# Gated cross-attention with a mixture of experts: VectorE's, GpSimd's and SyncE's steps of a loop turn in another order

## The chip, the cores and the metric

The kernel runs on one core of a Trainium2 chip. The metric is the device time of one launch in microseconds. The engines are named PE (TensorE), DVE (VectorE), ACT (ScalarE), POOL (GpSimd) and SP (SyncE, which here only issues DMAs). Each engine works through its own list of instructions in order, and engines are tied to each other by semaphores.

## The reference

32 sequences of 128 tokens, 256 features, 16 heads of 16, 8 experts with 1024 hidden features, all in 32 bits:

```python
x = x + tanh(g_xattn) * attention(layernorm(x), ctx, ctx, w_q, b_q, w_k, b_k, w_v, b_v, w_o, b_o)
# attention: causal softmax(q k^T / 4) v per head, over the 128 tokens of a row, then @ w_o.T + b_o
# ffn(x): logits = x @ Wr + br; top 2 of 8 experts; weights = softmax of the two logits
#         sum over them of weight * (gelu(x @ W1[e] + b1[e]) @ W2[e] + b2[e])
x = x + tanh(g_ffn) * ffn(layernorm(x), W1, b1, W2, b2, Wr, br)
```

## The kernel before

The launch has two parts. `attention_and_routing` does the attention, the second layer norm and the choice of experts for all 4096 tokens, and writes each normalised token into rows of a table in HBM (`xs_dram`) sorted by expert; on the side it turns the experts' weights into scaled pairs of 16 bit numbers. `experts` then runs over 39 tiles of 256 rows. All edits are in the first part.

The first part works in 16 groups g of two sequences (256 tokens). Each engine has a function `it(g, par, half, stays, stayed)` that writes out one turn of the loop, and `loop_over_groups` runs it for g = -2 to 17; `there(g)` says whether a group exists, so that the turns at both ends have only some of the steps. `par` is g mod 2 and chooses the buffer of a pair, `p1` = 1 - par, `g1` = g + 1. A turn has eight slots n = 0 to 7, one for each block of four heads of one sequence. Several groups are in work at once. In turn g:

- group g has its scores in slot n (PE, L906), their maxima for each row (DVE, L753), a cover, that is the mask with the maxima in it (POOL, `affine_select`, L502), the transposed scores with the cover taken off (PE, L964 and L966, two slots later), the exponentials (ACT, L591), and the product with the values (PE, L999, three slots later);
- group g + 1 is prepared. Keys: projection (PE, slot 1), the first of three 16 bit parts (ACT, `first_part`, L570), what is left of it (DVE, `rest`, L682, reads the PSUM bank PJB), the second part (ACT, L609), the third part (DVE, `third`, L694). Queries: the same from slot 3 on. The values' projection (PE, slot 2) overwrites PJB, so it waits for `rest` of the keys (`k_left`). SP copies each part as soon as it is made into the stacked layout that the scores read, six DMAs for the keys and six for the queries (L413);
- group g - 1 is finished: normalisation of the output (`normalise`, L702 and L703), output projection (PE, slots 0 and 4), the second residual (`residual`, L713, which reads `xb` = x + gated bias, made by POOL at L511), its variance, 1/std (POOL, L494), the norm (`norm2`, L722), transposes, and the router's product in slot 7, then logits, mask (L854) and shifted logits (L856);
- group g - 2 gets its places: exponentials, weights, counts (L789 to L806, slot 1), positions (L745, L747) and slots (L811 to L820, slot 2), and POOL scatters its rows by four indirect DMAs (L519);
- one layer of one expert's weights is loaded (SP, L399, into `stage`), squared and summed (ACT, L639, slots 3 to 6), and in the next turn scaled and split into a high half (ACT, L646, slots 1 to 4) and a low half (DVE, L763, four pieces of 512);
- slot 7 also takes the first layer norm's statistics of group g + 2 (DVE, L863 to L870), with 1/std on POOL (L528), and slot 0 of the next turn applies them (L770).

SP's order in a turn is: loads of x and context for group g + 2 (L359, L360; they wait until the buffers are free, that is for `xn_ready`, `xb_ready` and `cT_psum` of group g), the load of weights (it waits for the low halves of the turn before, `w_low`), the copies of keys and of queries, the store of the residual, and from group 8 on a store of the split weights. The order on each engine is written by hand.

## Time and profile before

| | us |
|---|---|
| median of 3 runs | 928.24 (926.72 to 928.42) |
| the profiled execution | 926.99 |
| its span, from the first to the last instruction | 925.2 |
| busy in it: PE, weight loads, DVE, ACT, POOL | 825.1, 743.3, 611.5, 441.2, 354.1 |

The attention part ends at about 454 us, the experts take the rest. In the first part the weights' sum of each turn (L842, end of slot 7) stands at 51.8, 79.2, 103.75 and so on to 430.9, once in each turn. A row of the timeline gives the start, the duration, the engine, line and operation, what it writes and reads, and in brackets how long the engine was idle just before and what ended that. Neighbouring instructions of DVE overlap a little, so one starts before the end of the last. An instruction that stands in its engine waiting for a port counts as busy.

### The profile page before, as it was taken

The numbers are of one execution on the slowest core, as the hardware profiler recorded it, in microseconds if no ns is written. First come the engines' busy times: TensorE is split into PE (matmuls) and PEld (weight loads), VectorE is DVE, ScalarE is ACT, GpSimd is POOL, SyncE is SP. The second block draws the span as 40 slices with busy tenths as digits, with TensorE's granted clock in tenths as the row PEclk, the third lists the DMA queues.
The fourth block names the chain that finished last, engine by engine and source line by source line (L and its number), as shares of the span: only waits on it lengthen the run. The fifth ranks groups of instructions, "written<-read, shape, count | busy, mean of one in ns | idle before, by whom it ended". The sixth has DMA issues, their size and how long they took to land. (4 is left out here: it accounts for less than half of the span.)

```text
span 925.2 us, 24761 instructions
## 1 busy us (share of the span) xinstructions
PE 825.1 (89%) x7472; PEld 743.3 (80%) x7473; DVE 611.5 (66%) x1492; ACT 441.2 (48%) x962; POOL 354.1 (38%) x365
## 2 busy tenths in 40 slices
PE   4599999999999999997259999999999999999990
PEld 3488888888888888887148999999998999999980
DVE  2368988899889989996635556555555555555550
ACT  2146555656555555554034444444455444444440
POOL 2233565554555555654301322332223223322232
PEclk9799999999999999999569999999999999999996
DMA  8876657667667887672577332233233332223222
GB/s 186 151 138 141 165 154 154 139 150 165 160 155 200 207 217 200 189 191 82 183 267 270 61 55 49 49 50 53 48 55 56 50 53 49 49 48 43 24 25 26
DMA packets 87947, 108.80 MB, mean 118 GB/s; under 512 B 12832, under 2 KB 81568, under 8 KB 85664
## 3 DMA queue, kind: packets, MB, share of 16 engines
q1 hardware_dynamic: 72448, 87.17, 37.3%
q0 software_dynamic: 14304, 19.15, 13.3%
q8 instruction: 60, 0.98, 0.4%
q10 hardware_dynamic: 1088, 1.11, 0.4%
q14 instruction: 47, 0.39, 0.2%
HBM read 46.82 MB, written 34.36 MB: 88 GB/s over the span
## 5 line engine op out<-in xcount | busy, mean ns | idle before, releaser
L1228 POOL DMA_INDIRECT out_rows<-yg,xs x78 | 128.0, 1641 | 330.4 <-ACT yg L1270 193.4
L1360 PE MATMUL bank<-xh,wts 128*128 128x256 f16 x1872 | 213.6, 275 | 0.0
L1376 PE MATMUL bank<-wts,hh 128*128 x1872 | 210.6, 273 | 0.0
L1360 PEld LDWEIGHTS bank<-xh,wts 128*128 x1872 | 184.6, 99 | 22.3
L1376 PEld LDWEIGHTS bank<-wts,hh 128*128 128x128 f16 x1872 | 183.2, 98 | 21.2
L1260 ACT ACTIVATE hf<-bank,b1t,gscale 128x256 f32<-128x256 f32 x312 | 154.3, 560 | 24.3 <-PE bank L1360 24.3
L502 POOL TENSOR_SCALAR_AFFINE_SELECT xs<-rowmax 128x512 bf16<-128x512 bf16 x128 | 96.0, 750 | 161.5 <-DVE rowmax L753 147.1
L999 PE MATMUL bank<-va,probs 128*128 128x102 f32 x1024 | 140.6, 279 | 3.8 <-DVE ao L703 3.5
L1270 ACT ACTIVATE yg<-yb,xs 128x256 f32<-128x256 f32 x78 | 35.4, 500 | 199.5 <-DVE yb L1309 184.1
L999 PEld LDWEIGHTS bank<-va,probs 128*128 128x128 f32 x1024 | 125.1, 193 | 5.5 <-issue 3.4
L1299 DVE SCALAR_TENSOR_TENSOR hh<-hf,hscale,hh 128x512 f16<-128x512 f32 x156 | 117.2, 752 | 5.6
L591 ACT ACTIVATE probs<-bank 128x512 f32<-128x512 f32 x128 | 76.4, 597 | 73.3 <-PE bank L966 53.9
L1309 DVE SCALAR_TENSOR_TENSOR yb<-bank,yscale,b_all 128x512 f32<-128x512 f32 x39 | 29.3, 750 | 109.0 <-PE bank L1376 109.0
L753 DVE TENSOR_REDUCE rowmax<-bank 128x4 bf16<-128x512 f32 x128 | 87.6, 685 | 16.3 <-PE bank L906 13.5
L1298 DVE TENSOR_SCALAR hh<-hf,hscale 128x512 f16<-128x512 f32 x156 | 75.5, 484 | 22.1 <-ACT hf L1260 15.6
L519 POOL DMA_INDIRECT token_rows<-pay,slots x64 | 71.7, 1121 | 22.2 <-DVE slots L816 10.8
L964 PE MATMUL bank<-negident,xs 128*128 128x128 bf16 x512 | 73.3, 220 | 6.7 <-POOL xs L502 6.7
L966 PE MATMUL bank<-wts 96*128 96x128 bf16 x512 | 73.5, 220 | 0.0
L1283 DVE SCALAR_TENSOR_TENSOR xh<-bank,xh 128x512 f16<-128x512 f32 x39 | 27.0, 692 | 67.3 <-ACT xh L1251 65.7
L906 PE MATMUL bank<-wts 128*128 128x128 bf16 x512 | 50.3, 221 | 16.7 <-DMA wts<-queries 14.6
L964 PEld LDWEIGHTS bank<-negident,xs 128*128 128x128 bf16 x512 | 49.9, 99 | 10.0 <-POOL xs L502 9.1
L906 PEld LDWEIGHTS bank<-wts 128*128 128x128 bf16 x512 | 40.4, 101 | 20.4 <-issue 17.3
(165 smaller groups left out, 1072.3 us busy)
## 6 DMA issues: line engine op xcount, KB each, us to landing
wts<-in_W SPq DMA_DIRECT2D x16, 1024.0 KB, 8.7
wts<-keys SPq DMA_DIRECT2D x96, 128.0 KB
wts<-queries SPq DMA_DIRECT2D x96, 128.0 KB
xs<-token_rows SPq DMA_DIRECT2D x39, 272.0 KB
split_weights<-wts SPq DMA_DIRECT2D x8, 1024.0 KB
wts<-split_weights SPq DMA_DIRECT2D x8, 1024.0 KB, 7.4
xin<-in_x SPq DMA_DIRECT2D x16, 256.0 KB, 2.8
cin<-in_ctx_in SPq DMA_DIRECT2D x16, 256.0 KB, 3.1
```

What stands on the lines that cost most here:

```text
L502: pool.affine_select(out=cover[n % 4][:, :, :], in_=rowmax[n % 2][:, :].unsqueeze(2).to_broadcast([P, 4, P]), compare_op=ALU.is_ge, fill=M ...
L591: act.activation(probs[q % 4][:, :, :].rearrange("p a q -> p (a q)"), TB[q % 2][:, :], ACT.Exp, scale=float(DK) ** -0.5).then_inc(exp_read ...
L753: dve.tensor_reduce(rowmax[n % 2][:, :], SB[n % 2][:, :].rearrange("p (a k) -> p a k", a=4), AX, ALU.max).then_inc(max_ready, 1)
L906: last = pe.matmul(ps[:, a * P:(a + 1) * P], qfull[par][:, h, tok], kfull[par][:, h, tok], start=True, stop=True)
L964: pe.matmul(ps[:, a * P:(a + 1) * P], cover[m % 4][:, a, :], negident[:, :], start=True, stop=False)
L999: last = pe.matmul(OB[:, h * VA:(h + WIDE) * VA], probs[m % 4][:, a, :], va[i][:, b, h, :].unsqueeze(1).to_broadcast([P, WIDE, VA]), start ...
L1228: pool.indirect_dma_start(out=out[:, :], out_offset=bass.IndirectOffsetOnAxis(ap=numbers, axis=0), in_=yg[m % 2][:, half, :], in_offset=No ...
L1260: last = act.activation(hf[:, c, :], HB[quarter][:, c % 2 * TILE:(c % 2 + 1) * TILE], ACT.Gelu, bias=b1t[:, bass.ds(e, 1), c], scale=gscal ...
L1298: step(dve.tensor_scalar(high, full, hscale[:, bass.ds(e, 1)], None, ALU.mult))
L1299: dve.scalar_tensor_tensor(out=hh[b][:, 1, c, :].rearrange("p c t -> p (c t)"), in0=full, scalar=hscale[:, bass.ds(e, 1)], in1=high, op0=A ...
L1360: last = pe.matmul(HB[c // 2][:, c % 2 * TILE:(c % 2 + 1) * TILE], wts[:, bass.ds(expert[1], 1), at:at + P], xh[b][:, xp, k, :], start=q = ...
L1376: last = pe.matmul(YB[b][:, half * D:(half + 1) * D], hh[b][:, hp, c, half * P:(half + 1) * P], wts[:, bass.ds(expert[0], 1), at:at + D], ...
```

## The change

- DVE: `rest` of the keys stands in slot 1 amid the routing steps of group g - 2, behind `esum`, instead of behind all of them (in turns without such a group it stays at its place).
- DVE: the four pieces of the low half lie in slots 3, 4, 5, 6 instead of 2, 3, 5, 6.
- DVE: `third` of the queries stands in slot 5 behind the maxima instead of at the end of slot 4.
- DVE: in turns 15 and later the second `normalise` stands in slot 2, ahead of the slots' steps, instead of slot 3.
- POOL: the sum x + bias is made in the group's own turn, ahead of slot 2's cover, instead of in slot 6 of the turn before.
- POOL: the third of the four indirect DMAs lies in slot 6 instead of slot 5.
- SP: the load of weights comes first in a turn, ahead of the loads of x and context.

```diff
--- before.py
+++ after.py
@@ -348,6 +348,18 @@
                     return a[bass.ds(g * (GT * P), GT * P), :].rearrange("(b p) d -> p b d", p=P)
 
                 def it(g, par, half, stays, stayed):
+                    if there(g):
+
+                        when(sp, there(g - 2), w_low, (g - 1) * 4)
+                        settled(sp)
+                        e = half
+                        if par == 0:
+                            src = W1[bass.ds(e, 1), :, :].rearrange("a (k p) n -> p (a k) n", p=P)
+                            dst = stage[0].rearrange("p (k n) -> p k n", k=KC)
+                        else:
+                            src = W2[bass.ds(e, 1), :, :].rearrange("a (k p) n -> p (a k) n", p=P)
+                            dst = stage[1].rearrange("p (k n) -> p k n", k=HC)
+                        sp.dma_start(dst, src).then_inc(w_staged[par], 16)
                     if there(g + 2):
 
                         when(sp, there(g), xn_ready, g + 1)
@@ -385,18 +397,6 @@
                         for half in range(2):
                             at = E * REG + half * P
                             load(xs_dram[at:at + P, :], padrow[:, :])
-                    if there(g):
-
-                        when(sp, there(g - 2), w_low, (g - 1) * 4)
-                        settled(sp)
-                        e = half
-                        if par == 0:
-                            src = W1[bass.ds(e, 1), :, :].rearrange("a (k p) n -> p (a k) n", p=P)
-                            dst = stage[0].rearrange("p (k n) -> p k n", k=KC)
-                        else:
-                            src = W2[bass.ds(e, 1), :, :].rearrange("a (k p) n -> p (a k) n", p=P)
-                            dst = stage[1].rearrange("p (k n) -> p k n", k=HC)
-                        sp.dma_start(dst, src).then_inc(w_staged[par], 16)
                     if there(g + 1):
                         for w, src, st, made, dst_ready in (
                                 (1, keys, kst, (k_first, k_second, keys_ready), kst_ready),
@@ -493,6 +493,14 @@
                             pool.wait_ge(var2_ready, (g - 1) * GT + b + 1)
                             pool.tensor_tensor(rs2[:, b:b + 1], mv2[:, b, 1:2], power[:, 0:1],
                                                ALU.pow).then_inc(rstd2_ready, 1)
+                        if n == 2 and there(g):
+
+                            arrived(pool, x_loaded, g, par)
+                            when(pool, there(g - 2), x2_ready, (g - 1) * GT)
+                            pool.wait_ge(bias_ready, 1)
+                            pool.tensor_tensor(xb[par][:, :, :], xin[par][:, :, :],
+                                               bo_all[:, :].unsqueeze(1).to_broadcast([P, GT, D]),
+                                               ALU.add).then_inc(xb_ready, 1)
                         if there(g):
 
                             pool.wait_ge(max_ready, g * QUADS + n + 1)
@@ -503,16 +511,8 @@
                                                in_=rowmax[n % 2][:, :].unsqueeze(2).to_broadcast([P, 4, P]),
                                                compare_op=ALU.is_ge, fill=MASKED, base=0, pattern=[[0, 4], [-1, P]],
                                                channel_multiplier=1).then_inc(cover_ready, 1)
-                        if n == 6 and there(g + 1):
-
-                            arrived(pool, x_loaded, g + 1, 1 - par)
-                            when(pool, there(g - 1), x2_ready, g * GT)
-                            pool.wait_ge(bias_ready, 1)
-                            pool.tensor_tensor(xb[1 - par][:, :, :], xin[1 - par][:, :, :],
-                                               bo_all[:, :].unsqueeze(1).to_broadcast([P, GT, D]),
-                                               ALU.add).then_inc(xb_ready, 1)
-                        if n in (3, 4, 5, 7) and there(g - 2):
-                            b, r = divmod((3, 4, 5, 7).index(n), 2)
+                        if n in (3, 4, 6, 7) and there(g - 2):
+                            b, r = divmod((3, 4, 6, 7).index(n), 2)
                             if n == 3:
                                 pool.wait_ge(slots_ready, g - 1)
                                 settled(pool)
@@ -735,7 +735,8 @@
                             dve.wait_ge(tanh_ready, 2)
                             dve.tensor_scalar(bo_all[:, :], bo_all[:, :], tgx[:, 0:1], None,
                                               ALU.mult).then_inc(bias_ready, 1)
-                        if n == 3 and there(g - 1):
+                        ending = isinstance(g, int) and g >= NG - 1
+                        if n == 3 and there(g - 1) and not ending:
                             normalise(g - 1, 1)
                         if n == 7 and there(g):
                             normalise(g, 0)
@@ -752,11 +753,13 @@
                             when(dve, n >= 2 or there(g - 1), cover_ready, g * QUADS + n - 1)
                             dve.tensor_reduce(rowmax[n % 2][:, :], SB[n % 2][:, :].rearrange("p (a k) -> p a k", a=4),
                                               AX, ALU.max).then_inc(max_ready, 1)
+                        if n == 5 and there(g1):
+                            third(g1, p1, n)
                         if n == 5 and there(g - 1):
                             norm2(g - 1, 1, p1)
-                        if n in (2, 3, 5, 6) and there(g - 1):
-
-                            k = (2, 3, 5, 6).index(n)
+                        if 3 <= n <= 6 and there(g - 1):
+
+                            k = n - 3
                             c = slice(512 * k, 512 * k + 512)
                             dve.wait_ge(w_high, g * 4 - 3 + k)
                             e = half - (1 - par)
@@ -790,7 +793,10 @@
                             for b in range(GT):
                                 step.later(dve.tensor_tensor_scan(cnt[:, b, :], ones8[:, :], msk16[:, b, :], 0.0,
                                                                   ALU.mult, ALU.add))
-                            step(dve.tensor_reduce(esum[:, :], em[:, :, :], AX, ALU.add))
+                            step.later(dve.tensor_reduce(esum[:, :], em[:, :, :], AX, ALU.add))
+                            if there(g1):
+                                rest(g1, n)
+                            step.wait()
                             step.later(dve.reciprocal(erec[:, :], esum[:, :]))
 
                             step.later(dve.tensor_tensor(cm[:, :, :], cnt[:, :, :], msk16[:, :, :], ALU.mult))
@@ -806,6 +812,8 @@
                             step(dve.tensor_tensor(sel[:, :, :, :], over_ranks(cm[:, :, :]),
                                                    rank1[:, :].unsqueeze(1).unsqueeze(3).to_broadcast([P, GT, 8, E]),
                                                    ALU.is_equal))
+                        if n == 2 and there(g - 1) and ending:
+                            normalise(g - 1, 1)
                         if n == 2 and there(g - 2):
 
                             step(dve.tensor_tensor(sel[:, :, :, :], sel[:, :, :, :], over_ranks(pos[:, :, :]), ALU.mult))
@@ -818,7 +826,7 @@
                                                      op1=ALU.add).then_inc(slots_ready, 1)
                             dve.wait_ge(slots_ready, g - 1)
                             step.later(dve.tensor_copy(all_slots[:, bass.ds((g - 2) * GT, GT), :], slots[par][:, :, :]))
-                        if n == 1 and there(g1):
+                        if n == 1 and not there(g - 2) and there(g1):
                             rest(g1, n)
                         if n == 2 and there(g1):
                             third(g1, p1, n)
@@ -834,8 +842,6 @@
                             rest(g1, n)
                         if n == 4 and there(g - 1):
                             residual(g - 1, 1, PJB, p1)
-                        if n == 4 and there(g1):
-                            third(g1, p1, n)
                         if n == 7 and there(g):
 
                             dve.wait_ge(w_total, g + 1)
```

## Rows read from the trace of the kernel before

**Rows 1.** Windows: length, busy PE, PEld, DVE, ACT, POOL; clock, DMA share, GB/s.
```profile
103.75:408.34 304.59, 287.34 (x2679) 262.67 (x2677) 275.17 (x793) 174.65 (x396) 166.46 (x193) 1.00 0.70 173
...
419.80:423.20 3.40, 3.40 (x24) 3.34 (x23) 1.52 (x3) 1.46 (x4) 1.88 (x3) 0.50 0.10 36
```

**Rows 2.** Groups by line, DVE, 20 to 425: busy us, mean ns, idle before.
```profile
L854 DVE TENSOR_TENSOR msk<-lg,mx 128x16 bf16<-128x16 f32 x14 | 14.3, 1022 | 0.5
...
L713 DVE SCALAR_TENSOR_TENSOR x<-bank,tgx,xb 128x256 f32<-128x256 f32 x29 | 13.9, 478 | 11.5 <-PE bank L887 11.5
...
L811 DVE TENSOR_TENSOR sel<-sel,pos 128x128 f32<-128x128 f32 x14 | 10.1, 720 | 0.0
...
L870 DVE TENSOR_SCALAR mv<-mv 128x2 f32<-128x2 f32 x15 | 5.0, 334 | 0.5
...
L672 DVE TENSOR_SCALAR mv<-mv 128x1 f32<-128x1 f32 x29 | 4.5, 154 | 1.0
...
L806 DVE TENSOR_TENSOR sel<-cm,rank 128x128 f32<-128x128 f32 x14 | 4.0, 284 | 0.0
```

**Rows 3.** Timeline, slots 6 and 7: start, duration, instruction, [idle before, releaser].
```profile
203.67 1.50 POOL L519 DMA_INDIRECT token_rows<-pay,slots  x1 [0.17 <-DVE rowmax L753]
...
205.80 1.27 POOL L511 TENSOR_TENSOR xb<-xin,bo_all 128x512 f32<-128x512 f32 x1
...
206.05 1.07 DVE L854 TENSOR_TENSOR msk<-lg,mx 128x16 bf16<-128x16 f32 x1
...
207.02 0.64 POOL L502 TENSOR_SCALAR_AFFINE_SELECT xs<-rowmax 128x512 bf16<-128x512 bf16 x1
```

**Rows 4.** Timeline, slots 1 and 2, of POOL, DVE and PE.
```profile
214.00 0.64 POOL L502 TENSOR_SCALAR_AFFINE_SELECT xs<-rowmax 128x512 bf16<-128x512 bf16 x1 [0.86 <-DVE rowmax L753]
...
214.93 0.15 DVE L796 TENSOR_TENSOR cm<-cnt,msk 128x16 f32<-128x16 f32 x1
...
215.81 0.88 DVE L682 SCALAR_TENSOR_TENSOR k_rest<-bank,bqk,keys 128x256 f32<-128x256 f32 x2
...
216.75 0.48 PE L887 MATMUL bank<-wv_sb,cT 128*128 128x256 f32 x1 [1.04 <-DVE k_rest L682]
```

**Rows 5.** Timeline, slots 4 to 7, of POOL, DVE and PE.
```profile
225.02 0.63 POOL L502 TENSOR_SCALAR_AFFINE_SELECT xs<-rowmax 128x512 bf16<-128x512 bf16 x1 [0.61 <-DVE rowmax L753]
...
225.39 0.48 DVE L713 SCALAR_TENSOR_TENSOR x<-bank,tgx,xb 128x256 f32<-128x256 f32 x1 [0.71 <-PE bank L887]
...
227.28 0.68 DVE L753 TENSOR_REDUCE rowmax<-bank 128x4 bf16<-128x512 f32 x1
...
227.88 0.41 DVE L722 TENSOR_SCALAR pay<-x,mv,rs 128x256 f32<-128x256 f32 x1
...
228.29 1.15 POOL L502 TENSOR_SCALAR_AFFINE_SELECT xs<-rowmax 128x512 bf16<-128x512 bf16 x1 [0.50 <-DVE rowmax L753]
...
229.50 0.23 PE L964 MATMUL bank<-negident,xs 128*128 128x128 bf16 x1 [0.48 <-POOL xs L502]
...
251.74 0.56 POOL L494 TENSOR_TENSOR rs<-mv,power 128x1 f32<-128x1 f32 x1
...
251.96 0.69 DVE L694 TENSOR_TENSOR queries<-q_rest,queries 128x512 bf16<-128x512 f32 x1 [0.31 <-issue]
```

**Rows 6.** Timeline, SP's copies of the queries, and the scores that read them.
```profile
222.97 5.03 SPq L413 DMA_DIRECT2D wts<-queries  x6
...
232.23 0.39 PE L906 MATMUL bank<-wts 128*128 128x128 bf16 x4
```

**Rows 7.** Timeline, turns 15 and 16, of DVE and PE.
```profile
418.66 0.26 DVE L702 RECIPROCAL rden<-bank 128x16 f32<-128x16 f32 x1
...
419.52 1.75 PE L999 MATMUL bank<-va,probs 128*128 128x102 f32 x8 [2.89 <-DVE ao L703]
...
425.00 0.48 DVE L713 SCALAR_TENSOR_TENSOR x<-bank,tgx,xb 128x256 f32<-128x256 f32 x1 [2.15 <-PE bank L887]
...
443.58 0.48 DVE L713 SCALAR_TENSOR_TENSOR x<-bank,tgx,xb 128x256 f32<-128x256 f32 x1 [2.67 <-PE bank L887]
```

## The prediction

> **What bounds the kernel now.** I read first the windows of the attention part, where all edits lie. Twelve turns of the loop take 304.59 us, 25.38 each; PE is busy 287.34 (23.95 a turn), DVE 275.17 (22.93), ACT 174.65, POOL 166.46, at granted clock 1.00 [rows 1]. With 2.45 us of DVE idle and 1.43 of PE idle a turn, neither engine alone is the bound; the two take turns at holding the loop. So I looked at who waits for whom, and at what DVE's busy time consists of.
>
> DVE waits in one place of each turn: the second residual sum (L713), in slot 4, waits 0.71 for PE's output projection [rows 5]; over the 29 of them it is 11.5 us, the second of each turn having nearly all of it [rows 2]. PE for its part had waited 1.04 for the rest of the keys before the value projection at 216.75 [rows 4], and from there it works without a wait over 0.3 up to the projection that DVE then lacks. So the chain is: DVE in slot 1 (routing, then the rest of the keys), PE in slots 2 to 4, DVE's residual sum. After it DVE runs in its own order, and PE waits 0.48 for a cover in slot 7 [rows 5].
>
> The second thing is time in which DVE counts as busy and does nothing. The comparison that makes the mask (L854, 128x16) takes 1.02 on average, where another small one (L870, 128x2) takes 0.33 and L672 (128x1) 0.15. It starts at 206.05 while POOL's bias sum runs (205.80 to 207.07) and ends 0.05 after that [rows 2, 3]. L811 (128x128) takes 0.72, where L806 of the same size takes 0.28, and L870 loses 0.17 in the same way [rows 2]. An operation that reads a PSUM bank and one SBUF tile loses nothing: L713 at 225.39 overlaps the select of 225.02 and takes its usual 0.48 [rows 2, 5]. It goes both ways: the select of 228.29 takes 1.15 instead of 0.64, because a weights' half (L763, 0.74) was under way behind L722 [rows 3, 5].
>
> **The change part by part**, for one turn, against the one that begins at 205.4.
>
> *Slots 2 to 4.* A weights' low half costs DVE 0.74 less the 0.08 by which neighbours overlap (L753 at 227.28 takes 0.68, the next starts 0.60 later), so 0.66 [rows 5]. The halves lie in slots 3, 4, 5, 6 instead of 2, 3, 5, 6. Between the routing and the second residual sum DVE still has two of them, but one now lies behind slot 4's maxima, in the 0.71 that DVE stood idle, and what comes before it (third part of the keys, second normalisation, maxima, values, rest of the queries) is 0.66 earlier. That pays only if PE's projection comes earlier too. It does: the rest of the keys, moved into the routing, ends near 215.55 instead of 216.7, and the value projection starts at about 215.75, as PE's work before it ends at 216.75 - 1.04 = 215.71 [rows 4]. PE then meets DVE's normalised output about 0.1 to 0.3 before it is there, and arrives at the residual sum 0.85 to 1.0 earlier; I leave DVE 0.07 of its wait. L811 gains as well: it starts right after slot 2's maxima, before POOL's select of that slot asks (a select starts 0.33 after its maxima end: 228.29 behind 227.96 [rows 5]), and its 0.44 of blocking goes. The slots' sum behind it then meets that select and loses about 0.15. Sum: 0.71 + 0.44 - 0.15 - 0.07 = 0.93; ends 0.4 (PE gives half of it) and 1.15.
>
> *Slot 5.* Before: third part of the queries, maxima (227.28), norm of the second half (L722, 227.88), weights' half [rows 5]. Now the maxima come first, then the third part, then the norm: the same work, but POOL meets it otherwise. POOL's rstd (L494, 0.56 at 251.74) lies behind slot 4's indirect DMA and now runs as the third part starts; the nearest row is the third part at 251.96, which found DVE idle for 0.31 beside such an L494 [rows 5]. I take 0.2 (ends 0 and 0.56, the whole L494). Then slot 5's select asks while the third part runs, and is granted before the norm, which waits for it: 0.64 less the overlap, 0.55 (ends 0 and 0.64; 0 if the norm asks first, as at 228.29, where the select stood behind L722 and L763). Sum -0.75; ends 0 and -1.2. PE's transposes of that norm come 0.5 later by this, while slot 5's cover comes about 0.8 earlier after the residual sum: PE's wait of 0.48 goes from the one place to the other, at no cost.
>
> A rule of the Trainium skill speaks here. By "SBUF — State Buffer", section "Who interferes with whom", GpSimd and a VectorE instruction in a two-port mode or with two SBUF inputs share ports, and whichever issues first keeps them for its whole length. The trace agrees for L854 (end 0.05 behind L511's), and not for the third part beside L494, 0.31 of a possible 0.56. By the rule alone slot 5 would cost 1.1 and the turn would gain 0.4 instead of 0.8.
>
> *Slot 7.* The bias sum (1.27) leaves the place before the mask. POOL's order there is now: slot 6's select, an indirect DMA (slot 5's, moved to slot 6), slot 7's select; before, that DMA (203.67, 1.50) lay ahead of slot 6's select [rows 3]. Counting these through, slot 7's select starts just before the mask and holds it 0.36, against 0.84 now (1.02 less 0.18). L870 gets free of its DMA (0.17), and the tiny L856 of the select at 207.02 (0.07). Sum 0.84 - 0.36 + 0.17 + 0.07 = 0.72; ends 0.44 (a whole select before the mask) and 1.08 (nothing before it).
>
> *Slot 1.* The bias sum now follows slot 1's select, from about 214.65 to 215.92 [rows 3, 4]. The rest of the keys (0.80 to the next start, PSUM source, so not held) runs beside it from 214.75 to 215.55. The next with two SBUF operands, L796, is then held until 215.9: it took from its start to L682's 0.88 to finish the routing [rows 4], so that this ends at 216.74, where routing and rest ended at 215.81 + 0.80 = 216.61. Loss 0.13; ends +0.05 (the step between esum and its reader is filled) and -0.6 (if ACT's first part of the keys came late, more of the 1.27 would lie bare).
>
> *SP's queue.* The weights' load now stands before the loads of x and context, and those wait for the bias sum of their own turn: they go out at about 216.1, nearly 9 us later, and the first copies of the keys behind them at about 217. That costs nothing where I can see it: the last copy of the keys waits for the third part anyway (about 219.9), x is read in slot 7, and the copies of the queries start near 222 as now. The last copy of the queries goes out behind a third part that is 0.8 later after the residual sum. Now the six are issued from 222.97 to 228.00, and PE's scores that read them run at 232.23 [rows 6]: 4.2 between. It becomes 3.5 to 4.
>
> *Per turn:* 0.93 - 0.75 + 0.72 - 0.13 = 0.77, taken as 0.8: a turn of 24.6. PE's busy 23.95 [rows 1] is below that, and caps the gain at 1.4. Turns 2 to 14 have all parts: 13 x 0.8 = 10.4. The first two have only some: 0.8.
>
> *The end.* In turns 15 and 16 the second normalisation comes before L811 and the slots; in turn 15 right behind slot 2's maxima, at about 416.4 instead of 418.66. PE sat idle 2.89 for it until 419.52 and then ran at a granted clock of 0.50 from 419.8 to 423.2 [rows 1, 7]. From 419.52 to the residual sum at 425.0 took 5.5, where the same piece of a steady turn takes about 3.9. With PE idle below 1 us I expect no drop: 2.3 + 1.6 = 3.9 earlier, less 0.4 for slot 5's blocking. In turn 16 the normalisation is 1.85 earlier, and the residual sum, which waited until 443.58 [rows 7], about 2.1, its projection still at the low clock. Sum 5.6; ends 3.5 and 7.
>
> Sum: 10.4 + 0.8 + 5.6 = 16.8. The profiled execution took 926.99 (span 925.2 and 1.8 around it): 910.2. The median of the three runs is 928.24, 1.25 above it: 911.4. **Forecast 911.4.** The experts' part (from about 454 on) has no edit and moves as a block.
>
> **Rivals.** *Slot 5's queue eats it* (0.2): L494 holds the third part in full, a select holds the norm, and PE's transposes, the router's product and the weights' sum follow late; slot 5 costs 1.2 and the turn gains 0.3: 13 x 0.3 + 0.8 + 4.7 = 9.4, 919. This is the skill's rule taken whole (the same page). For it: L854's row; against it: the one row with L494 first. *POOL's instructions fall kindly* (0.14): the norm asks before the select, the mask before slot 7's; the gain reaches PE's bound, 1.4: 18.2 + 0.8 + 6 = 25, 903. *The copies arrive late: slower* (0.05): twelve copies and the loads of x and context lie between 216 and 231 in SP's queue. If the last copy of the queries lands over 3.7 after its issue, PE waits at slot 0's scores and DVE with it, each us beyond costing one a turn; from 1.3 us on (16.8 / 13) the kernel is slower than before; at 2 us 13 x 2 - 16.8 = 9, 937. Against it: the weights' load has left that stretch. *Nothing moves* (0.03): waits only change their names, since PE's 23.95 and its fixed waits for ACT already make the period; the end's gain goes into SP's delay: 927. The forecast's own case has 0.58.
>
> **Numbers.** About 0.2%, 1.9 us, is what a measurement of this kernel can tell from no change. Faster 0.58 + 0.2 + 0.14, of which I give 0.01 to same: 0.91; same 0.04; slower 0.05. Range: a turn's gain of 0.4 to 1.4 with the end's 3.5 to 7 makes 9.5 to 25: 903 to 919; 920 on the upper side for part of the first rival. The last two rivals and the tails of the others stay out, under 0.2 together.
>
> **What would show it.** The turn's length near 24.6; L713's second wait under 0.2; PE's wait before the value projection gone; L854's mean at 0.3 to 0.7; L811 at 0.28; L722 near 0.95 in most turns; L796 near 0.45; no half clock at 420; L906 not waiting for the queries' copies. The forecast is wrong if L722 stays at 0.41 (then the turn is shorter), if L854 is held by something longer than a select, or if PE waits at slot 0's scores.

## The result, and the profile after

The changed kernel takes **917.02 us** (median of 6 runs, 915.74 to 920.7), the kernel before 927.73 in the runs beside it: ratio 0.9895, interval 0.9874 to 0.9917, about 10 us faster. The forecast was 911.4, with a range of 903 to 920. The profiled execution took 917.29, with a span of 915.5 (926.99 and 925.2 before), so 9.7 us are to be found in the traces where the forecast had 16.8.

I split the span at the weights' sum that ends each turn (L842 before, L848 after), at the second residual sum (L713) and at the table that ends the first part.

| stretch | before, us | after, us | earlier | forecast |
|---|---|---|---|---|
| start to the end of turn 1 | 79.20 | 79.49 | -0.3 | 0.8 |
| turns 2 to 14 (13 turns) | 329.14 | 323.14 | 6.0 | 10.4 |
| turn 15 to the table | 50.05 | 46.35 | 3.7 | 5.6 |
| the table to the end (experts) | 466.81 | 466.52 | 0.3 | 0 |

The windows of the profile (length, busy PE, PEld, DVE, ACT, POOL, then clock, DMA share, GB/s), the kernel after, to hold against [rows 1]:

```profile
104.36:402.63 298.27, 285.75 (x2678) 263.05 (x2677) 267.55 (x793) 171.27 (x396) 155.80 (x193) 1.00 0.81 177
419.80:423.20 3.40, 2.56 (x27) 2.47 (x28) 3.37 (x7) 1.48 (x4) 1.48 (x3) 1.00 0.10 39
433.50:464.20 30.70, 7.92 (x36) 5.76 (x37) 13.91 (x65) 1.79 (x4) 8.44 (x9) 0.50 0.63 218
```

Twelve turns take 298.27, 24.86 each instead of 25.38. DVE is busy 7.6 us less in them. The half clock at 420 is gone; the long one before the experts (last row) is there in both kernels. Now the groups by line, DVE, 104 to 403 us of after (busy us, mean ns, idle before), to hold against [rows 2]; L854 and L811 are now L860 and L819:

```profile
L722 DVE TENSOR_SCALAR pay<-x,mv,rs 128x256 f32<-128x256 f32 x24 | 13.5, 563 | 0.0
L713 DVE SCALAR_TENSOR_TENSOR x<-bank,tgx,xb 128x256 f32<-128x256 f32 x24 | 11.5, 479 | 1.1 <-PE bank L893 0.5
...
L682 DVE SCALAR_TENSOR_TENSOR q_rest<-bank,bqk,queries 128x256 f32<-128x256 f32 x24 | 10.5, 479 | 7.3 <-ACT queries L570 7.2
...
L860 DVE TENSOR_TENSOR msk<-lg,mx 128x16 bf16<-128x16 f32 x12 | 7.5, 629 | 0.4
...
L819 DVE TENSOR_TENSOR sel<-sel,pos 128x128 f32<-128x128 f32 x12 | 3.4, 281 | 0.0
```

DVE's wait before L713 is nearly gone. A new one stands at the rest of the queries, for ACT's first part: 7.2 us. The mask is down from 1.02 to 0.63, L819 to 0.28, and L876 (L870 before) to 0.17. L722 is up: every second one is held by 0.32. The rest of the lost time shows in PE's waits (who waits for whom, the total, how often, the longest), 104 to 400 us of after:

```profile
PE bank L1005 <- DVE ao L703: 3.7, 12, 0.4
...
PE bank L912 <- DMA wts<-queries: 2.4, 3, 0.9
...
PE bank L912 <- issue: 0.6, 1, 0.6
```

The wait before the value projection is gone (5.6 us in 11 before in the same view). L912 is the scores' first product (L906 before), and its waits for the queries' copies are new. The timeline shows one turn with such a wait and one without (SP's issues of the copies and PE's product, behind turns 3 and 6):

```profile
120.49 5.77 SPq L413 DMA_DIRECT2D wts<-queries  x6
...
131.08 0.39 PE L912 MATMUL bank<-wts 128*128 128x128 bf16 x4 [0.87 <-DMA wts<-queries]
```

```profile
201.11 0.55 SPq L413 DMA_DIRECT2D wts<-queries  x1
```

```profile
205.45 0.39 PE L912 MATMUL bank<-wts 128*128 128x128 bf16 x4
```

From the end of the last issue to the product it is 3.8 us in the second (205.45 - 201.66) and 4.8 in the first (131.08 - 126.26); before it was 4.2 in every turn [rows 6]. The copies need up to a microsecond longer than PE now gives them. By the starts of the weight loads, PE stood 1.13, 1.06, 0.18, 1.02, 0.08 and 0.81 us at this place behind turns 3, 5, 7, 11, 12 and 13, 4.28 in all, and nothing behind the other seven. I call them **stalls** below, with their sum over turns 1 to 13. Before, they are zero. The turn behind a stall is numbered one higher: the stall behind turn 3 lies at the start of turn 4.

### The profile page after: what moved, and what is told of

It reads as the page before. It is cut to its first block and busy times, and to the rows that moved or that the text cites. A ratio compares the mean times of both kernels' runs of the same rounds, so it can differ in the third digit from the quotient of the medians.

```text
span 915.5 us, 24759 instructions
## 1 busy us (share of the span) xinstructions
PE 821.4 (90%) x7472; PEld 742.2 (81%) x7473; DVE 602.9 (66%) x1492; ACT 437.5 (48%) x962; POOL 341.1 (37%) x365
## 5 line engine op out<-in xcount | busy, mean ns | idle before, releaser
L510 POOL TENSOR_SCALAR_AFFINE_SELECT xs<-rowmax 128x512 bf16<-128x512 bf16 x128 | 93.4, 730 | 165.6 <-DVE rowmax L754 152.5
L519 POOL DMA_INDIRECT token_rows<-pay,slots x64 | 66.0, 1031 | 22.3 <-issue 11.2
L912 PE MATMUL bank<-wts 128*128 128x128 bf16 x512 | 50.1, 221 | 19.3 <-DMA wts<-queries 16.9
L912 PEld LDWEIGHTS bank<-wts 128*128 128x128 bf16 x512 | 39.7, 100 | 24.0 <-issue 20.8
L972 PEld LDWEIGHTS bank<-wts 96*128 96x128 bf16 x512 | 50.2, 98 | 3.8 <-issue 0.3
```

The costliest lines, as they stand in the source:

```text
L510: pool.affine_select(out=cover[n % 4][:, :, :], in_=rowmax[n % 2][:, :].unsqueeze(2).to_broadcast([P, 4, P]), compare_op=ALU.is_ge, fill=M ...
L912: last = pe.matmul(ps[:, a * P:(a + 1) * P], qfull[par][:, h, tok], kfull[par][:, h, tok], start=True, stop=True)
L972: last = pe.matmul(ps[:, a * P:(a + 1) * P], kst[i][:, h, tok], qst[i][:, h, tok], start=False, stop=True)
```

## Experiments

All undo one part of the change or do some parts alone. "Turns" is the stretch of turns 2 to 14, "turn" the mean of the twelve of them that the windows cover. These two and the stalls are read from the one profiled execution of each kernel, which isn't always near the median: that of e1 took 923.71, that of e7 915.2.

| kernel | median, us | ratio (interval) | turns | turn | stalls |
|---|---|---|---|---|---|
| before | 926 to 928 | 1 | 329.14 | 25.38 | 0 |
| after | 917.02 | 0.9895 (0.9874 to 0.9917) | 323.14 | 24.86 | 4.3 |
| e1_w_later | 920.08 | 0.9927 (0.9897 to 0.9956) | 327.91 | 25.25 | 7.0 |
| e2_third_back | 915.84 | 0.989 (0.986 to 0.9921) | 322.61 | 24.84 | 8.4 |
| e3_rest_back | 929.17 | 1.0035 (1.0016 to 1.0054) | 333.78 | 25.71 | 1.9 |
| e4_halves_back | 923.3 | 0.9966 (0.9949 to 0.9983) | 328.39 | 25.29 | 5.5 |
| e5_ctx_early | 916.04 | 0.9883 (0.9855 to 0.9911) | 321.57 | 24.73 | 1.8 |
| e6_bias_back | 916.95 | 0.9893 (0.9856 to 0.9929) | 322.17 | 24.77 | 0 |
| e7_ctx_early_third_back | 913.74 | 0.985 (0.9813 to 0.9887) | 318.18 | 24.47 | 1.8 |
| e8_end_back | 921.38 | 0.994 (0.9915 to 0.9964) | 325.47 | 25.05 | 5.8 |
| e9_dma_back | 919.38 | 0.9925 (0.9899 to 0.9951) | 323.77 | 24.91 | 7.0 |
| e10_bias_third_back | 913.5 | 0.9856 (0.983 to 0.9882) | 318.26 | 24.48 | 0.1 |
| e11_only_dma | 928.69 | 1.0021 (1.0003 to 1.0039) | 329.61 | 25.42 | 0.2 |
| e12_before_four_parts | 913.0 | 0.9846 (0.9816 to 0.9876) | 318.28 | 24.48 | 0.7 |

### The parts that carry the gain: e3, e4

e3 puts the rest of the keys back behind all the routing steps:

```diff
-    step.later(dve.tensor_reduce(esum[:, :], em[:, :, :], AX, ALU.add))
-    if there(g1):
-        rest(g1, n)
-    step.wait()
+    step(dve.tensor_reduce(esum[:, :], em[:, :, :], AX, ALU.add))
...
-    if n == 1 and not there(g - 2) and there(g1):
+    if n == 1 and there(g1):
         rest(g1, n)
```

> The changed kernel with the rest of the keys back behind the whole routing of slot 1. Theory: PE waits again about 1.0 before the values' projection, DVE again waits for PE at the queries' rest or the second residual sum, and the bias sum has nothing of the routing's free time beside it: the routing's L796 is held in full (about 1.0). Each of 13 turns gets 0.8 to 1.3 longer: 928 to 932, as slow as before the change or slower. Rival (the move of the rest pays nothing, since PE's stalls elsewhere take its place): within 2 us of 917.

Measured 929.17, as the theory had it: without this part the change makes the kernel 3 us slower. PE's wait for the rest of the keys is back (waits, 104 to 413 us of this kernel), and the bias sum now falls on a small DVE operation of slot 1:

```profile
PE bank L890 <- DVE k_rest L682: 8.3, 12, 1.2
```

```profile
216.36 1.28 POOL L501 TENSOR_TENSOR xb<-xin,bo_all 128x512 f32<-128x512 f32 x1
...
216.61 1.06 DVE L799 TENSOR_TENSOR cm<-cnt,msk 128x16 f32<-128x16 f32 x1
```

L799 ends at 217.67, 0.03 behind the bias sum. Its mean is 0.95 over 12, where the changed kernel has 0.36 for the same line (L802), since there the rest of the keys, which reads PSUM, lies beside most of the bias sum.

e4 puts the low halves back to slots 2, 3, 5 and 6:

```diff
-    if 3 <= n <= 6 and there(g - 1):
+    if n in (2, 3, 5, 6) and there(g - 1):
...
-        k = n - 3
+        k = (2, 3, 5, 6).index(n)
```

> The changed kernel with the weights' low halves back in slots 2, 3, 5, 6. Theory: DVE stands idle again about 0.7 before the second residual sum and all before it comes 0.66 later, so PE's product with the values waits for the normalisation: a turn of 25.1 to 25.3 where it is 24.6, 13 x 0.5 = 6.5, with a little less at the end, 921 to 924. Rival (PE's chain is the bound and DVE has slack there in every turn): 917 to 918.

Measured 923.3, as expected. DVE waits for PE's output projection again (the waits of DVE, 104 to 400 us):

```profile
DVE x L713 <- PE bank L893: 8.2, 12, 0.8
```

### What makes PE wait at the scores: e1, e5, e2, e7

My first theory was that the load of weights (1 MB), now ahead in SP's queue, crowds the copies. e1 puts it a few us later, behind the point where the buffer of the context is free:

```diff
+    when(sp, there(g + 1), cT_psum, g + 2)
+    settled(sp)
     e = half
```

> The changed kernel with one more wait on SP: the load of the experts' weights goes out only when PE has done slot 0's transposes of the context, that is after the scores of slot 0, about 3 us later in each turn. In the changed kernel PE stood about 1 us at slot 0's scores in five of twelve long turns (they took 25.3 instead of 24.6), with the last copy of the queries issued 5.2 us before. Theory A (the weights' load, 1 MB, put ahead, crowds the copies of the queries): the stalls go, 4 us less than the changed kernel, about 913. Theory B (the copies are late because the third part and the keys' copies are issued late, whoever loads what behind them): stalls stay, 917 as the changed kernel, at most 1 us off. The load is still early enough for its reader in slot 3.

Measured 920.08 with stalls of 7.0 instead of 4.3: the theory fell, and the median isn't within 1 us of 917 either, as the other theory had it. (Of waits of 0.8 or more there are four by the weight loads, not five.) Two of its stalls, 1.71 and 1.54 us long, each came with a stretch at half clock (a window of e1):

```profile
382.40:385.80 3.40, 3.40 (x18) 2.85 (x17) 2.34 (x7) 0.01 (x1) 1.54 (x2) 0.51 0.93 306
```

The next suspect stands in the queue behind. Since SP works in order, the load of the context (256 KB) waits behind the load of x, which waits for the bias sum of slot 2, though the context's own buffer is free 12 us earlier (e5 below issues that load at 202.32). SP's issues in one turn of after:

```profile
214.70 0.37 SPq L371 DMA_DIRECT2D xin<-in_x  x1
215.16 0.42 SPq L372 DMA_DIRECT2D cin<-in_ctx_in  x1
215.84 3.84 SPq L413 DMA_DIRECT2D wts<-keys  x6
220.84 5.44 SPq L413 DMA_DIRECT2D wts<-queries  x6
```

Both loads, 512 KB, now go out about a microsecond ahead of the twelve copies (1.1 and 0.7). e5 takes the context's load to the head of the turn; x, which must wait, stays:

```diff
+    if there(g + 2):
+        when(sp, there(g), cT_psum, g + 1)
+        settled(sp)
+        sp.dma_start(cin[par][:, :, :], group_rows(ctx_in, g + 2)).then_inc(c_loaded[par], 16)
...
     sp.dma_start(xin[par][:, :, :], group_rows(x, g + 2)).then_inc(x_loaded[par], 16)
-    sp.dma_start(cin[par][:, :, :], group_rows(ctx_in, g + 2)).then_inc(c_loaded[par], 16)
```

> The changed kernel, but the load of context (256 KB) no longer stands with the load of x behind the bias sum; it goes first in SP's turn, ahead of the weights (it only needs the earlier transposes). Theory C (the loads of x and context, 512 KB just ahead of the twelve copies, are the crowd: in the turns in which PE stood at slot 0's scores only 1585 to 1642 of the 2048 KB issued since them had moved when the last copy of the queries was issued, in the others 1713 to 1799): 256 KB less in the stretch, no stall at slot 0's scores, all turns near 24.6: 3 to 4 us less than the changed kernel, 913 to 914. Theory B (the copies take 5 us from their own number and the place of their issue): stalls stay in four or five turns, 917.

The stalls fell from 4.3 to 1.8 and the turns by 1.6 us, but the median only by 1.0, less than expected and within what the medians scatter. e2 puts the third part of the queries back to the end of slot 4:

```diff
-    if n == 5 and there(g1):
-        third(g1, p1, n)
...
+    if n == 4 and there(g1):
+        third(g1, p1, n)
```

> The changed kernel with the queries' third part back at the end of slot 4, ahead of slot 5's maxima; all else as changed. My account of slot 5 says that the norm (L722) is then not held any more (0.41 instead of 0.72), residual sum to weights' sum 5.95 instead of 6.35, and the last copy of the queries goes out 0.6 earlier, so that most stalls at slot 0's scores go: turn 24.3 to 24.5, 911 to 913. Rival: PE's own chain is the bound now, and its wait only goes from the transposes of the norm (0.41) back to slot 5's cover (0.69): then the turn stays, and only the stalls of the copies are gained, 914; if those are not from the third part's place either, 917.

Measured 915.84. From the residual sum to the turn's end it is 5.95 again, as expected. The shortest turns, behind stalls of 0.24 or less, are 24.37 and 24.38 here, and 24.53 in after, yet the stalls doubled to 8.4 instead of going away. The longest, 1.74 us at 377.6, also cost clock (a window of e2):

```profile
377.40:380.80 3.40, 3.21 (x15) 2.68 (x16) 1.71 (x7) 0.00 (x0) 1.57 (x3) 0.50 0.99 413
```

So both edits were made together in e7:

> Context's load early and the queries' third part back at the end of slot 4. With theory C the ten stalls (0.84 each) of the third part's kernel at slot 0's scores go for the most part, and its shorter slot 5 (5.95 instead of 6.33 from the residual sum to the weights' sum) comes through: turn 24.2 to 24.3, 909 to 911. Rival (PE's wait for slot 5's cover, 0.69, is part of PE's own chain and sets the turn at 24.6): 913 to 914.

Measured 913.74, above the 909 to 911 expected; the turns take 318.18. Against e2 this differs in the place of the one load alone: 4.4 us of turns, stalls 8.4 to 1.8. Of the 4.4, 2.65 are turn 14 alone (27.03 to 24.38), in which e2's clock fell, and the medians are 2.1 apart with intervals that overlap. Against e5 it differs in the third part alone: 3.4 us. Of the 5.0 us by which the turns are shorter than in after, the span shows 2.1: 1.3 went before the end of turn 1 and 1.4 behind the table. The median lies in the rival's 913 to 914, and the turn of 24.47 lies between the 24.2 to 24.3 of the theory and the 24.6 of the rival; no run explains the rest.

### The bias sum, and who holds the mask: e6, e9, e11

e6 puts the bias sum back to slot 6 of the turn before; with it the loads of x and context go out early:

```diff
-    if n == 2 and there(g):
-        arrived(pool, x_loaded, g, par)
...
+    if n == 6 and there(g + 1):
+        arrived(pool, x_loaded, g + 1, 1 - par)
...
```

> The changed kernel with the bias sum back in slot 6 of the turn before; SP's order stays as changed, so that weights, x and context all go out about the end of slot 7. Theory of slot 7: the mask (L854 before) is held about 0.9 to 1.0 again instead of 0.45, nothing is held amid the routing (0.25 back), and no stall at slot 0's scores, as the loads are out of the copies' way (-4 us): together about +0.3 a turn less 4: 916 to 919. Rival (the mask's wait is hidden, because PE is the bound there): only the copies' gain remains, 913.

There are no stalls, as expected. But the mask was not held: the expectation that it would take 0.9 to 1.0 fell (timeline of e6, slots 6 and 7):

```profile
203.29 1.26 POOL L511 TENSOR_TENSOR xb<-xin,bo_all 128x512 f32<-128x512 f32 x1
...
204.61 0.17 DVE L860 TENSOR_TENSOR msk<-lg,mx 128x16 bf16<-128x16 f32 x1
```

The bias sum ends at 204.55, just before the mask asks. With one indirect DMA less in slot 5, POOL comes to it 1.1 us earlier in the turn than before. What DVE wins in slot 7 it then waits in slot 0, 0.7 to 1.3 us in each of turns 3 to 14, for the 1/std of POOL's L528.

The median of 916.95 lies in the span expected, but the account behind it did not hold. All 4.3 us of stalls are gone, and the thirteen turns are only 1.0 shorter than in after. Turn by turn: behind stalls of 1.13, 1.06, 1.02 and 0.81, turns 4, 6, 12 and 14 of after are 0.61, 0.57, 0.50 and 0.20 longer than those of e6, 1.9 in all. Turn 10, which has no stall in either kernel, takes 24.85 and 24.86. Turns 5, 7, 11 and 13 are 0.14 to 0.42 longer in e6. So **a stall costs half of its length or less** where the clock holds. Turn 4 in both (windows of after and of e6):

```profile
129.32:154.73 25.41, 23.80 (x226) 21.89 (x225) 22.08 (x68) 14.23 (x33) 13.06 (x17) 1.00 0.76 167
```

```profile
129.60:154.40 24.80, 23.80 (x226) 21.95 (x225) 22.01 (x67) 14.23 (x33) 12.89 (x17) 1.00 0.68 160
```

For the mask, e9 put the DMA back and left the bias sum in slot 2:

```diff
-    if n in (3, 4, 6, 7) and there(g - 2):
-        b, r = divmod((3, 4, 6, 7).index(n), 2)
+    if n in (3, 4, 5, 7) and there(g - 2):
+        b, r = divmod((3, 4, 5, 7).index(n), 2)
```

> The changed kernel with one thing undone: the group's third indirect transfer on GpSimd is issued in slot 5 again instead of slot 6; the bias sum stays in its own group's slot 2. Theory: it is this transfer, not the bias sum, that held the mask of slot 7 in the kernel before. With it in slot 5, slot 5's scan starts 1.0 us later on GpSimd, the selects of slots 6 and 7 end later, and the mask of slot 7 lasts 0.9 to 1.06 us again instead of 0.17 to 0.62. The stretch from the last score to slot 0's maximum (3.17 us after, 3.63 before) goes to 3.5 to 3.6, the turn from 24.86 to 25.1 to 25.4, the whole to 920 to 923 us. Rival: the bias sum was what mattered and the transfer's place is indifferent; then the mask stays at 0.6 or below, the turn stays at 24.9 and the whole at 916 to 918.

This theory fell as well, in the other direction (timeline of e9):

```profile
203.91 0.64 POOL L510 TENSOR_SCALAR_AFFINE_SELECT xs<-rowmax 128x512 bf16<-128x512 bf16 x1 [1.05 <-DVE rowmax L754]
...
204.16 0.42 DVE L860 TENSOR_TENSOR msk<-lg,mx 128x16 bf16<-128x16 f32 x1
```

The mask takes 0.42, less than in after (0.63), for the select of slot 7 is further on when it asks. Before had both, the DMA in slot 5 and the bias sum in slot 6, and only both together put the bias sum beside the mask: either move alone frees most of it. Mask and turn (24.91) came out as the rival had them. The median of 919.38 is 2.4 above that of after, with intervals that overlap. In the profiled execution the turns lost 0.6, and 2.3 came behind the table, where nothing is edited; I leave the difference open.

e11 does the same move alone on the kernel before:

> The kernel before with one thing done alone: the group's third indirect transfer moves from slot 5 to slot 6. Theory: the mask of slot 7 is no longer held (0.17 instead of 1.06 us), the stretch from the last score to slot 0's maximum goes from 3.63 to about 2.8 us, and the turn from 25.38 to 24.6 to 25.0; the whole to 917 to 923 us. Rival: VectorE is early but waits for TensorE, whose own wait before the value projections (0.73 us a turn) takes it up; the turn stays at 25.3 to 25.4, the whole at 926 to 927 us.

Measured 928.69, no gain. Here are the groups of DVE and the waits of DVE and PE, 104 to 400 us of e11:

```profile
L770 DVE TENSOR_SCALAR xn<-xin,mv,rs 128x256 f32<-128x256 f32 x24 | 12.1, 542 | 12.4 <-POOL rs L528 12.4
...
L854 DVE TENSOR_TENSOR msk<-lg,mx 128x16 bf16<-128x16 f32 x12 | 2.1, 175 | 0.4
```

```profile
DVE xn L770 <- POOL rs L528: 12.4, 12, 1.3
DVE x L713 <- PE bank L887: 7.9, 11, 0.8
```

```profile
PE bank L887 <- DVE k_rest L682: 6.2, 12, 0.7
```

The mask takes 0.17 and slot 0's maximum comes 0.9 earlier, and then DVE waits 1.0 each turn for POOL's 1/std, whose place in the queue is now behind two indirect DMAs. The rival said the turn would stay, and it did; the wait that took the gain is another one than it named. So **what is won in slot 7 is not a gain by itself**: in slots 0 and 1 DVE had that much in hand.

### Four parts without the others: e10, e12

e10 is the changed kernel with both the edits of e2 and of e6. e12 comes from the other side, the kernel before with four parts: rest amid the routing, halves in 3 to 6, the third indirect DMA in slot 6, the order at the end. They differ in SP's order alone: in e10 the load of weights is first.

> The changed kernel with two things undone together: the bias sum is back in slot 6 of the turn before, and the third part of the queries' rest is back in slot 4. All else, the order of the loads on SP's queue too, is as changed. Undone alone, the first gave a turn of 24.77 and no wait of TensorE at slot 0's scores, the second 24.84 with such waits. Theory: the waits at slot 0's scores are what hid the gain of the second, and with the bias sum back they are gone, so both gains add: a turn of 24.2 to 24.5, no wait at the scores over 0.2 us, 910 to 913 us. Rival: with the third part back in slot 4, TensorE's wait for the weight cover of slot 5 (0.69 us a turn before) sets the turn again: 24.6 to 24.8, 914 to 917 us.

> The kernel before with four parts of the change: the rest of the keys amid the routing, the halves of the weights in slots 3 to 6, the third indirect transfer in slot 6 and the order at the end. Left as before are the bias sum in slot 6, the third part of the queries' rest in slot 4 and the order of the loads on SP's queue. Theory: the order of the loads costs nothing as long as the bias sum stays where it was, so this gives what the changed kernel gives with bias sum and third part back, within 1 us: 910 to 913 us, a turn of 24.2 to 24.5. Rival: with the old order all loads come later in the turn, their packets lie beside the queries' copies, and TensorE waits at slot 0's scores in some turns: 914 to 917 us.

Measured 913.5 and 913.0, both with a turn of 24.48, and all thirteen turns agree within 0.01, as 24.63 and 24.64 or 24.39 and 24.38. The theory holds for both in the turn and in the stalls; 913.5 lies 0.5 above its figure. With the bias sum in slot 6, the place of the load of weights costs nothing, and no stall is left beyond 0.5. Window of e12:

```profile
104.24:397.96 293.72, 282.91 (x2679) 261.50 (x2677) 258.45 (x793) 172.85 (x396) 161.64 (x193) 1.00 0.76 179
```

What PE still waits for is above all slot 5's cover, which it waited for before too (its waits in e12, 104 to 400 us):

```profile
PE bank L970 <- POOL xs L502: 5.7, 12, 0.5
```

e12 is the fastest of all by its median, 4.0 below after, with intervals that just touch; in the turns it is 4.9 shorter. It, e10 and e7 can't be told apart.

### The end: e8

```diff
-    ending = isinstance(g, int) and g >= NG - 1
+    ending = False
```

> The changed kernel without its special order in the last turns: the second normalisation of turns 15 and 16 stands in slot 3 again. Forecast was 5.6 for the end, of which the traces show 3.7 from the last full turn to the tile table. Theory: all of that hangs on this edit (PE's idle 2.9 before the products of slot 3, and the drop of the clock to 0.50 behind it): 920.5 to 922.5. Rival (half of it comes from the order of the halves in slots 3 and 4, which alone brings the normalisation 0.66 forward and fills DVE's wait): 918.5 to 919.5.

Measured 921.38, in the expected span, but its trace gives only part of it to the end. The idle time and the half clock are back:

```profile
416.22 1.11 PE L1005 MATMUL bank<-va,probs 128*128 128x102 f32 x8 [2.63 <-DVE ao L703]
```

```profile
417.80:421.20 3.40, 3.40 (x19) 3.22 (x17) 1.35 (x2) 3.09 (x8) 2.69 (x4) 0.51 0.11 41
```

Turn 15 takes 22.21 us here and 20.63 in after: 1.6 for this edit. From there to the table it is 25.80 and 25.72, the same. Another 2.3 us of its profiled execution lie in turns 2 to 14, where a stall of 1.70 behind turn 13 made a turn of 26.98. So 1.6 is shown, and the median's 4.4 is not explained in full. Of the end's 3.7 the edit gives 1.6 and not all, as the theory had it; the halves, which the rival named, give 0.2 (e4 takes 46.59 from turn 15 to the table). The other 1.8 came after turn 15, and no run takes it apart. It is within what the end varies by: e1, e3 and e10, which have this edit, ran 6.8 us at half clock about the end of turn 15 and took 28.2 to 28.3 from there to the table.

## Why the prediction was right and where it was wrong

Each turn is measured here in four stretches: from its start to slot 0's maxima (slot 7's work of the turn before), to the positions (slot 1), to the second residual sum (slots 2 to 4), and to its end (slot 5).

| stretch, sum of turns 2 to 14 | before, us | after, us | gain | forecast |
|---|---|---|---|---|
| slot 7 | 46.64 | 40.98 | 5.7 | 9.4 |
| slot 1 | 91.47 | 90.61 | 0.9 | -1.7 |
| slots 2 to 4 | 113.29 | 109.23 | 4.1 | 12.1 |
| slot 5 | 77.75 | 82.32 | -4.6 | -9.8 |

The sizes of the forecast were read off turn 7, whose length of 25.94 is the longest of the thirteen (mean 25.32).

**Slots 2 to 4 (0.93): right in some turns, mean 0.31.** In turn 5 the stretch went from 8.79 to 7.86, 0.93. DVE's wait, L819's blocking and PE's wait went as told. In turn 4, which begins with a stall, the same stretch went from 8.72 to 8.92: PE is late, so is ACT's first part of the queries, and DVE stands 1.12 before L682. But the stalls aren't all of it. Turn 9 has none before it and keeps a wait of 0.97, with a stretch of 8.54:

```profile
269.92 0.88 DVE L682 SCALAR_TENSOR_TENSOR q_rest<-bank,bqk,queries 128x256 f32<-128x256 f32 x2 [0.97 <-ACT queries L570]
```

Turns 2 and 8, with stalls of 0 and 0.18 before them, have waits of 1.12 and 1.21, and so has turn 14 of e5 without any stall, 1.21. There PE's work, not DVE's, sets the time of the residual sum. The forecast took what DVE wins as won in every turn.

**Slot 1 (-0.13): about right in that turn.** Turn 5 has 7.29 and 7.34 from slot 0's maxima to the positions. The rows are as counted:

```profile
213.11 1.27 POOL L501 TENSOR_TENSOR xb<-xin,bo_all 128x512 f32<-128x512 f32 x1
213.16 0.86 DVE L682 SCALAR_TENSOR_TENSOR k_rest<-bank,bqk,keys 128x256 f32<-128x256 f32 x2
...
214.02 0.40 DVE L802 TENSOR_TENSOR cm<-cnt,msk 128x16 f32<-128x16 f32 x1
...
214.71 1.91 PE L893 MATMUL bank<-wv_sb,cT 128*128 128x256 f32 x8
```

L802 ends at 214.42, 0.04 behind the bias sum; 0.45 was forecast and the mean is 0.36.

**Slot 5 (-0.75): the term was mis-sized, -0.40** (mean -0.35). From the residual sum to the turn's end it is 5.95 before and 6.35 after in nearly every turn. Timeline of after:

```profile
224.58 0.58 POOL L494 TENSOR_TENSOR rs<-mv,power 128x1 f32<-128x1 f32 x1
...
224.96 0.68 DVE L694 TENSOR_TENSOR queries<-q_rest,queries 128x512 bf16<-128x512 f32 x1
...
225.37 0.77 POOL L510 TENSOR_SCALAR_AFFINE_SELECT xs<-rowmax 128x512 bf16<-128x512 bf16 x1 [0.21 <-PE bank L972]
...
225.56 0.72 DVE L722 TENSOR_SCALAR pay<-x,mv,rs 128x256 f32<-128x256 f32 x1
...
226.33 0.44 PE L887 MATMUL bank<-ident,pay 128*128 128x128 f32 x2 [0.16 <-DVE pay L722]
```

I had taken 0.2 for the third part behind L494: it is not held at all, 0.68 beside an L494 that ends 0.20 into it, and so in all thirteen turns. I had taken 0.55 for the norm behind the select: it is held 0.32, as it starts when the select is already under way, so that L722 takes 0.72 where 0.95 was forecast. By the Trainium skill, "SBUF — State Buffer", section "Who interferes with whom", whoever issues first keeps the shared ports for the whole instruction. The trace agrees for L799 and L802, which end 0.03 and 0.04 behind the bias sum; beside the 128x1 instruction L494 it does not show it. The first rival, which took that rule whole, gave 919, nearer to the 917 measured than the forecast, but by a mechanism that did not occur: luck. Nor did the second: PE's busy time was not reached by any kernel, and it is no fixed bound either, with 23.95 a turn before, 23.81 in after and 23.58 in e12. (The upper end of the range, 25, counts 6 for the end where its sentence says 7.) The fourth, that waits only change their names, is true of e11 and not of the whole change.

**Slot 7 (0.72): measured 0.43** in turn 5 (3.50 to 3.07), and 0.44 on average. The mask is held by nearly a whole select, since the two start together:

```profile
205.31 0.65 POOL L510 TENSOR_SCALAR_AFFINE_SELECT xs<-rowmax 128x512 bf16<-128x512 bf16 x1
205.37 0.63 DVE L860 TENSOR_TENSOR msk<-lg,mx 128x16 bf16<-128x16 f32 x1
```

This is the lower end that the forecast named (0.44). That it was a term of the sum at all was too simple: by e11 it is worth nothing alone, and e12 and e7 have the same thirteen turns (318.28 and 318.18), though slot 7's stretch is 4.7 us shorter in e12.

The four together make 0.93 - 0.05 - 0.40 + 0.43 = 0.91 in turn 5, which went from 25.52 to 24.62, where 0.77 was forecast. Of the thirteen turns seven are between 24.53 and 24.74, as forecast.

**The step that failed, SP's queue: "That costs nothing where I can see it".** The time from the last issue to the scores was forecast well (3.5 to 4, measured 3.8), and that PE would wait if the copy took over 3.7 from its issue was the condition of the rival. What was wrong is the judgement that the copies would keep their pace because the load of weights had left. e1 shows, and e10 with e12, that it isn't this load that matters. What counts is that the loads of x and context moved from 6 us ahead of the keys' copies to right before them. PE then waits up to 4.8 from the end of the last issue for it. That the loads do it is shown by two pairs that differ in the place of the context's load alone: e7 against e2 (stalls 8.4 to 1.8, turns 4.4 shorter) and e5 against after (4.3 to 1.8, 1.6 shorter). How the load slows the copies was not measured.

The stalls sum to 4.3 us, and the turns lack 4.4 (10.4 less 6.0), but that the two agree is chance. Against e6, which has no stalls, the turns behind them lost 1.9 us, 0.15 a turn over the thirteen. So the rival came true in its mechanism and not in its price, which took a microsecond of wait for one of turn. The other 2.5 are in the terms above: a turn behind a stall of 0.18 or less is 24.53 to 24.96 where 24.5 was forecast (25.32 less 0.8), since slots 1 to 4 give 4.9 us and not 10.4, while slot 5 costs 5.2 less than forecast and slot 7 gives 3.7 less.

e12's thirteen turns take 318.28, and the forecast had 329.14 - 10.4 = 318.7. That agreement is luck too, and no check on the sum: e12 has neither the move of the third part nor that of the bias sum. Its four stretches, in the order of the table, gain 10.3, -9.7, 9.9 and 0.4, where the forecast has 9.4, -1.7, 12.1 and -9.8. What e12 does show is that four of the seven parts are enough for the turn that was forecast for all.

**The end (5.6): measured 3.7.** The first part was right: no drop of the clock at 420, and the second residual sum of turn 15 comes 13.5 us into the turn instead of 16.7 (L713 at 416.11 and 425.00, turns from 402.63 and 408.34), 3.2 earlier. Then 1.3 went again, so that turn 15 gained 1.9 where 3.5 was forecast, at a place that the forecast did not look at:

```profile
415.53 1.50 POOL L519 DMA_INDIRECT token_rows<-pay,slots  x1 [0.18 <-DVE rowmax L754]
417.05 0.65 POOL L510 TENSOR_SCALAR_AFFINE_SELECT xs<-rowmax 128x512 bf16<-128x512 bf16 x1
417.86 0.98 POOL L519 DMA_INDIRECT token_rows<-pay,slots  x1 [0.17 <-issue]
418.87 0.58 POOL L494 TENSOR_TENSOR rs<-mv,power 128x1 f32<-128x1 f32 x1
```

```profile
416.11 0.48 DVE L713 SCALAR_TENSOR_TENSOR x<-bank,tgx,xb 128x256 f32<-128x256 f32 x1
419.49 0.71 DVE L722 TENSOR_SCALAR pay<-x,mv,rs 128x256 f32<-128x256 f32 x1 [1.41 <-POOL rs L494]
```

The residual sum is early, but POOL is still in its two indirect DMAs, and the norm waits 1.41 for the 1/std behind them: an edit that moves one engine ahead must be followed into the next engine's queue. The first two turns were to gain 0.8 and lost 0.3; over all the kernels run, the end of turn 1 lies anywhere from 78.3 to 81.9, so that term can't be tested. Turn 16 and what follows gained 1.8 of the 2.1 forecast.

## What to carry to other kernels

A step that is moved takes with it what waits for it in an in-order DMA queue, and everything behind that: look up where each transfer behind it was issued before, and leave a transfer whose buffer is free ahead of one that must wait. Removed blocking is worth what the next engine in the loop lets through; a single edit on the kernel before (e11) tells that more cheaply than a sum of stages. A wait that a trace shows isn't its price: hold the same turn against one without the wait (4.3 us of stalls cost 1.9). A change in seven parts should be undone part by part: the kernel without three of these is 4.0 faster by its median, 4.9 in the turns, and the intervals just touch.

## What was not expected of the hardware

- The last of twelve copies of 128 KB within SBUF lands within 3.8 us of its issue's end or only at 4.8 (turns 6 and 3 of after), with the same two loads issued right before the twelve in both. Of turns 2 to 13 of after, stalls of 0.8 to 1.1 lie behind those that issue all twelve within 10.2 to 10.6 us (3, 5, 11 and 13; turn 7, with 10.4, has 0.18), and there is 0.08 or less behind those that take 10.9 to 11.5. In e5 it doesn't hold (11.3 with a stall of 0.76, 11.1 with none), and whether it is the cause wasn't tested.
- A wait of 1.5 to 1.7 us of PE amid full work came with 3.4 us at half clock in four cases (two in e1, one in e2, one in e8), and such a turn takes 27.0 to 27.5 us instead of 24.4 to 25.4. Once, in e4, it came with one of 1.18; a wait of 1.49 in e3 and several of 1.0 to 1.4 had none. The spread of the runs goes with it: of e1's eight, the three slowest (923.71 to 924.59) have a mean granted clock of 0.955 to 0.956 and the fastest (915.05) 0.965.
- An operation of DVE with two SBUF operands isn't held by a POOL instruction on a 128x1 tile that began before it (L694 beside L494, 0.68 in all of turns 2 to 14 of after and 0.69 without one), and is held to the end by one on 128x512 (L799, 1.06 instead of 0.15). Spans on POOL are rough, so that L494 may be done with its operands before its row ends.
